# Layer 0's transfer queue reordered: third context and batch 1's queries and keys first, X and the loads for the layer's end later

## The chip, the cores and the metric

The kernel runs on one core of one Trainium2 chip. The metric is device time in microseconds (us) of one launch. The core has five instruction streams: PE (TensorE: matmuls; its weight loads are listed apart as PEld), DVE (VectorE), ACT (ScalarE), POOL (GpSimd) and SP (SyncE), which here issues all transfers. A transfer issued by SP is carried out by the core's 16 DMA engines; SP goes on at once, and whoever needs the data waits on a semaphore that the transfer raises when it has landed.

## The reference

Four layers of different kinds run one after the other on x (8 x 100 x 512), with one context ctx (8 x 361 x 512) for all. Only layer 0 is touched by this change. Cut to what matters:

```python
# layer 0: B = 8 batches, 32 query heads in 8 groups of 4, head size 16
q = x @ Wq + bq                       # (8, 100, 512)
k = ctx @ Wk + bk                     # (8, 361, 128)
v = ctx @ Wv + bv                     # (8, 361, 128)
scores = q . k / 4 + mask             # per batch and group: 4*100 query rows by 361 keys
attn = softmax(scores)
out = (attn . v) @ Wo + bo            # (8, 100, 512)
x = layernorm(out + x) * gamma + beta
# layers 1 to 3 (a recurrence, a cross attention, two cross attentions with an MLP) follow
```

## The kernel before, in words

`gqa_layer` is layer 0. Its attention is `grouped_attention`, the function that the change edits. It holds the projections' weights in SBUF, makes the queries of all eight batches at the start (`make_queries`, twelve units; high and low parts `qh` and `ql`, the low part kept in the memory of `outT`), and then runs over the batches b = 0 to 7.

A batch has 25 score tiles of 128 query rows (`TILES`), numbered n over all batches, i within one. Per tile PE makes the scores (L651 to L656), DVE adds the mask and takes the maximum (L550), ACT exponentiates (L474), PE transposes (L594), ACT or DVE copies the turned tile out of PSUM (L458, L298), and later PE multiplies with the values (L606, L613). Between the tiles of batch b, PE also makes the keys of batch b+1 (L575, at i = 1 to 4) and its values (L584, at i = 13 to 18), from `ctx`, which has two buffers: batch b's context is in `ctx[:, b % 2]`.

What orders the work around the change is SP's queue, written out by hand. SP executes its list in order, and where it says `wait_ge` everything behind waits too. Its helpers are:

- `load_context(b)` (L303) and `load_mask(b)` (L306): 724 KB and 722 KB from HBM.
- `store_queries(i)` (L357): writes the query parts of batch 0 (i = 0), batches 1 to 3 (i = 1) or 4 to 7 (i = 2) to HBM. `stack_queries(b)` (L312) reads six pieces of batch b's queries back into `qs`, stacked as the score matmul wants them.
- `stack_keys(b)` (L319, L324): waits for the keys of b (`k_done`), writes their two parts to HBM, **waits for these to land**, and reads six pieces back into `ks`.
- `store_output(b, quad)` (L332, L335): waits for `y_done`, writes half of the batch's output into `outT` and its row sums to HBM.
- `pack_sums(b)` (L340): waits until both halves have landed and reads the sums back as 128 x 25. DVE takes their reciprocal (`invert_sums`, L517), which stands in DVE's list between tiles i = 23 and 24 of batch b+1.
- `widen_inverse(b)` (L345, L351): waits for the reciprocals, writes them to HBM, waits for the landing, reads them back in eight broadcasts. POOL then scales the output rows (`scale_rows`, L422).

PE's first tile of a batch waits for that batch's `qs`, `ks`, and for `only_done`, two small products of POOL (L440).

Not part of the attention itself are `X` (the input rows, 1600 KB, needed for the residual sum after the attention) and `late`, four tiles for the layer's end:

```python
late = [(bias[:], a["L0_bo"]), (Wo[:], by_chunks(a["L0_Wo"])), (gamma[:], a["L0_gamma"]), (beta[:], a["L0_beta"])]
```

POOL adds the bias to `X` in eight pieces (L436), in its turn for b == 2, ahead of that batch's `only` products.

Of the kernel before, what the change touches and what calls it, by code (L numbers as in the profile page):

```python
# [12 lines left out]
B, L, C = 8, 100, 512  # L13
# [174 lines left out]
TILES = 1 + BLOCKS * KV0  # L188
# [6 lines left out]
def grouped_attention(nc, a, X, ident, columns, column, qh, ql, Wk, Wv, bv, heads_of, ctx, outT, late, last_out, queries, keys,  # L195
# [19 lines left out]
    with Scope(nc, "ga") as sc:  # L215
# [28 lines left out]
        query_out = [sc.sem(f"query_out{i}") for i in range(len(SPANS))]  # L244
# [56 lines left out]
        def _(sp):  # L301
            def load_context(b):
                sp.dma_start(ctx[:, b % 2], ctxT[b]).then_inc(ctx_in[b % 2], 16)  # L303

            def load_mask(b):
                sp.dma_start(maskb[:, b % 2], mask[b]).then_inc(mask_in[b % 2], 16)  # L306

            def stack_queries(b):
                for e in range(2):
                    for slot in range(SLOTS):  # L310
                        row = (e * SLOTS + slot) * D0
                        sp.dma_start(qs[row:row + D0, b % 2, :, e].bitcast(F32),  # L312
                                     queries[Q_PART[slot]].rearrange("(p e d) b n -> e d b p n", e=2, d=D0)[e, :, b]).then_inc(
                                         qs_in[b % 2], 16)

            def stack_keys(b):
                sp.wait_ge(k_done, b + 1)
                for part, k in enumerate((kh, kl)):
                    sp.dma_start(keys[b % 2, part], k[:, b % 2].bitcast(F32)).then_inc(keys_out[b % 2], 16)  # L319
                sp.wait_ge(keys_out[b % 2], 32 * (b // 2 + 1))  # L320
                for e in range(2):
                    for slot in range(SLOTS):
                        row = (e * SLOTS + slot) * D0
                        sp.dma_start(ks[row:row + D0, b % 2].bitcast(F32),  # L324
                                     keys[b % 2, K_PART[slot]].rearrange("(p e d) s -> e d p s", e=2, d=D0)[e]).then_inc(
                                         ks_in[b % 2], 16)

            def store_output(b, quad):
                sp.wait_ge(y_done, QUADS * b + quad + 1)
                for j in range(4):  # L330
                    row = (4 * quad + j) * D0
                    sp.dma_start(outT[row:row + D0, b].rearrange("d h l -> d (h l)"),  # L332
                                 y[32 * j:32 * j + D0, quad, :]).then_inc(y_out[quad], 16)
                if b + 1 < B:
                    sp.dma_start(row_sums[b, 4 * quad:4 * quad + 4, :], y[D0:P:32, quad, :]).then_inc(y_out[quad], 16)  # L335

            def pack_sums(b):
                for quad in range(QUADS):
                    sp.wait_ge(y_out[quad], 80 * (b + 1))
                sp.dma_start(packed[:, b % 2], row_sums[b].rearrange("g n -> (g n)").rearrange("(p k) -> p k", k=NS)).then_inc(  # L340
                    packed_in, 16)

            def widen_inverse(b):
                sp.wait_ge(inverse_done, b + 1)
                sp.dma_start(inverses[b].rearrange("g n -> (g n)").rearrange("(p k) -> p k", k=NS), inverse[:, b % 2]).then_inc(  # L345
                    inverse_out, 16)
                sp.wait_ge(inverse_out, 16 * (b + 1))
                if b >= 2:
                    sp.wait_ge(scaled, b - 1)
                for g in range(KV0):  # L350
                    sp.dma_start(wide[g * D0:(g + 1) * D0, b % 2], inverses[b, g:g + 1].broadcast_to([D0, HG * L])).then_inc(wide_in, 16)  # L351

            def store_queries(i):
                first, end = SPANS[i]
                sp.wait_ge(query_low, CC * (i + 1))
                for part, q in enumerate((qh, ql)):
                    sp.dma_start(queries[part, :, first:end, :], q[:, first:end].rearrange("p b c l -> p b (c l)").bitcast(F32)).then_inc(  # L357
                        query_out[i], 16)
# [17 lines left out]
            load_context(1)  # L376
            load_mask(1)
            store_queries(1)
            sp.dma_start(X, a["x"].rearrange("b l c -> l b c")).then_inc(X_in, 16)
            store_queries(2)  # L380
            for tile, source in late:
                sp.dma_start(tile, source).then_inc(late_in, 16)
            for i in (1, 2):
                sp.wait_ge(query_out[i], 32)
            sp.wait_ge(tails_kept, 4)
            for b in range(B):
                if b and b + 1 < B:
                    sp.wait_ge(masked_done, TILES * b)
                    load_mask(b + 1)
                if b + 1 < B:  # L390
                    if b:
                        sp.wait_ge(score_full, TILES * b)
                    stack_queries(b + 1)
                if b:
                    store_output(b - 1, 0)
                if b + 1 < B:
                    stack_keys(b + 1)
                if b:
                    store_output(b - 1, 1)
                    pack_sums(b - 1)  # L400
                if b + 2 < B:
                    sp.wait_ge(value_full, b + 2)
                    load_context(b + 2)
                if b:
                    widen_inverse(b - 1)
            store_output(B - 1, 0)
            store_output(B - 1, 1)
            sp.wait_ge(late_in, 16 * len(late))
# [1 line left out]
        @block.gpsimd  # L410
        def _(pool):
            nc.gpsimd.memset(qs[:].bitcast(F32), 0.0).then_inc(stack_clear, 1)

            def keep_tails(first, end, units):
                pool.wait_ge(query_low, units)
                for part, q in enumerate((qh, ql)):
                    nc.gpsimd.tensor_copy(tail[:, part, first:end], q[:, first:end, HG - 1, L - LEFT:L].bitcast(F32)).then_inc(tails_kept, 1)

            def scale_rows(b):
                rows = outT[:, b].rearrange("p h l -> p (h l)")  # L420
                pool.wait_ge(wide_in, 16 * KV0 * (b + 1))
                nc.gpsimd.tensor_tensor(rows, rows, wide[:, b % 2], ALU.mult).then_inc(scaled, 1)  # L422

            pool.wait_ge(heads_in, 16)
            for b in range(B):
                if b == 0:
                    keep_tails(0, 1, CC)
                    pool.wait_ge(tails_kept, 2)
                if b == 1:
                    keep_tails(1, B, len(UNITS))  # L430
                    pool.wait_ge(tails_kept, 4)
                if b == 2:
                    pool.wait_ge(X_in, 16)
                    pool.wait_ge(late_in, 16 * len(late))
                    for i in range(B):
                        nc.gpsimd.tensor_tensor(X[:, i, :], X[:, i, :], late[0][0], ALU.add).then_inc(biased, 1)  # L436
                if b >= 2:
                    pool.wait_ge(score_full, TILES * (b - 2) + 1)
                for part in range(2):
                    nc.gpsimd.tensor_tensor(only[:, b % 2, part],  # L440
                                            tail[:, part, b:b + 1, :].broadcast_to([P, KV0, LEFT]),
                                            heads_of[:].rearrange("p (g a) -> p g a", a=1).broadcast_to([P, KV0, LEFT]),
                                            ALU.mult).then_inc(only_done, 1)
                if b >= 2:
                    scale_rows(b - 2)
            scale_rows(B - 2)
# [1565 lines left out]
class Heads:  # L2012
# [51 lines left out]
    def load_context(self, sp, n):  # L2064
        if n >= 2:
            sp.wait_ge(self.y_full, CC * (n - 1))
        b, rows = n % B, STILES[2][1]
        sp.dma_start(self.x[:, n % 2, :, 0:2].bitcast(F32), self.ctx_parts[b, :, :, 0:2]).then_inc(self.x_in[n % 2], 16)
        sp.dma_start(self.x[0:rows, n % 2, :, 2].bitcast(F32), self.ctx_parts[b, 0:rows, :, 2]).then_inc(self.x_in[n % 2], 16)
# [1052 lines left out]
```

## Time and profile before

| | us |
|---|---|
| Time before, median of 3 runs | 2667.86 |
| lowest and highest of the 3 | 2667.09, 2668.03 |
| the profiled execution's own time | 2664.75 |
| its span, first to last instruction | 2663.0 |
| PE busy in the span | 2457.7 (92%) |
| DVE, ACT, POOL busy | 1385.2, 1151.1, 753.3 |

Layer 0's attention takes roughly the first 270 us of the span. All positions in time below are us from the start of the span. In a timeline a row gives the start, the duration, the engine (SPq is SP's queue of issued transfers, the duration then that of the issuing), the line in the kernel, what is written from what, and in brackets how long the engine was idle before and who ended that.

### The profile page before, as it was taken

What the parts mean: (1) busy time and instruction counts of PE and PEld (TensorE: products, weight loads), DVE (VectorE), ACT (ScalarE), POOL (GpSimd) and SP (SyncE); (2) the same over time, 40 slices, a digit from 0 to 9 for tenths busy, and PEclk for the clock granted to TensorE, in tenths of its full rate; (3) what the DMA queues carried; (4) which work ended last, traced back from release to release, by engine and by line L of the source; (5) the groups of instructions that cost most, each with busy time, mean ns of one, the idle gap of its engine ahead of it and who ended that gap; (6) DMA issues with size and microseconds to landing.
All of it is one profiled execution on the core that took longest, in us unless ns stands there. A gap on an engine that the chain in (4) does not pass through costs nothing. (4 is left out here: it accounts for less than half of the span.)

```text
span 2663.0 us, 37768 instructions
## 1 busy us (share of the span) xinstructions
PE 2457.7 (92%) x13976; PEld 2162.7 (81%) x13976; DVE 1385.2 (52%) x2360; ACT 1151.1 (43%) x2473; POOL 753.3 (28%) x386
## 2 busy tenths in 40 slices
PE   7998689989999689899899999979999999999698
PEld 5675434479896457799899999979998999999698
DVE  4666631278885633233366665633334556664632
ACT  3786212233333432223476666622246666664320
POOL 1100322252220450442143342406204243431300
PEclk9999879999998799899999999999999999999799
DMA  7552253589994157434876665625287566663300
GB/s 234 131 135 67 84 211 113 135 249 237 240 234 154 67 179 241 143 137 158 298 238 211 202 208 177 196 86 184 107 298 254 189 205 215 218 198 110 115 16 25
DMA packets 237306, 459.14 MB, mean 172 GB/s; under 512 B 90588, under 2 KB 133620, under 8 KB 236356
## 3 DMA queue, kind: packets, MB, share of 16 engines
q1 hardware_dynamic: 237124, 456.73, 55.2%
q8 instruction: 112, 1.84, 0.3%
q14 instruction: 70, 0.57, 0.1%
HBM read 345.46 MB, written 119.37 MB: 175 GB/s over the span
## 5 line engine op out<-in xcount | busy, mean ns | idle before, releaser
L2007 PE MATMUL att_ring<-ca_pp,att_arena 128*128 128x400 f32 (+1 forms) x2304 | 431.3, 345 | 11.3 <-issue 9.0
L2007 PEld LDWEIGHTS att_ring<-ca_pp,att_arena 128*128 128x128 f32 (+1 forms) x2304 | 417.6, 189 | 18.1 <-issue 17.9
L2077 POOL TENSOR_TENSOR att_arena<-att_arena 128x1448 fp32r<-128x1448 f32 x64 | 212.3, 3317 | 611.7 <-ACT att_arena L2084 611.7
L2007 PE MATMUL att_ring<-att_arena,qk_wh 128*128 128x362 f32 x1024 | 256.4, 332 | 0.0
L2693 DVE TENSOR_TENSOR ca_yl<-att_ring,att_arena 128x400 fp32r<-128x400 f32 x256 | 146.6, 573 | 189.0 <-ACT att_arena L2651 189.0
L2007 PE MATMUL att_ring<-att_arena,qk_wl 128*128 128x362 f32 x512 | 173.2, 338 | 18.5 <-POOL att_arena L2264 18.2
L2007 PEld LDWEIGHTS att_ring<-att_arena,qk_wh 128*128 128x128 f32 x1024 | 185.5, 192 | 0.0
L2651 ACT ACTIVATE att_arena<-att_ring 128x400 fp32r<-128x400 f32 x256 | 128.8, 503 | 84.2 <-PE att_ring L2007 84.1
L2090 ACT ACTIVATE att_kstage<-att_score,att_shift 100x362 f32<-100x362 f32 x256 | 143.7, 562 | 43.4 <-DVE att_shift L2103 43.4
L1075 ACT ACTIVATE rec_stage<-rec_fbank,rec_columns 128x361 f32<-128x361 f32 x128 | 72.1, 563 | 197.3 <-PE rec_fbank L2007 196.6
L2007 PE MATMUL att_score<-att_arena 128*100 128x362 f32 x768 | 144.4, 338 | 0.0
L550 DVE CUSTOM_DVE_ANT_0 ga_masked<-ga_score,ga_maskb 128x361 f32<-128x361 f32 x200 | 103.4, 530 | 62.3 <-PE ga_score L656 52.3
L2007 PE MATMUL att_ring<-att_arena,ca_woh 128*128 128x400 f32 x512 | 135.0, 345 | 0.0
L2095 ACT ACTIVATE att_kstage<-att_kstage,att_share 100x362 f32<-100x362 f32 x256 | 132.2, 606 | 5.2 <-DVE att_share L2108 5.2
L2645 ACT ACTIVATE ca_pp<-att_ring 128x400 fp32r<-128x400 f32 (+1 forms) x192 | 83.0, 511 | 108.3 <-PE att_ring L2745 103.3
L2394 DVE TENSOR_SCALAR att_kstage<-att_ring,att_columns 128x361 f32<-128x361 f32 x64 | 37.9, 592 | 173.9 <-PE att_ring L2007 173.9
L2007 PEld LDWEIGHTS att_score<-att_arena 128*100 128x100 f32 x768 | 124.6, 169 | 1.1
L474 ACT ACTIVATE ga_probs<-ga_masked,ga_top 128x361 f32<-128x361 f32 x200 | 116.3, 595 | 15.5 <-DVE ga_top L550 15.3
L1161 DVE TENSOR_TENSOR_SCAN rec_work<-rec_wb,rec_work 128x1600 f32<-128x1600 f32 x32 | 117.8, 3682 | 2.6 <-DMA rec_wb<-kept_decay 2.6
L2101 DVE TENSOR_REDUCE att_top<-att_score 100x1 f32<-100x362 f32 x256 | 117.5, 521 | 1.2 <-PE att_score L2007 1.2
L2323 ACT ACTIVATE att_kstage<-att_ring,att_columns 128x361 f32<-128x361 f32 x64 | 36.1, 563 | 185.6 <-PE att_ring L2007 185.6
L2007 PEld LDWEIGHTS att_ring<-att_arena,qk_wl 128*128 128x128 f32 x512 | 98.3, 192 | 22.0 <-issue 11.8
(408 smaller groups left out, 5880.1 us busy)
## 6 DMA issues: line engine op xcount, KB each, us to landing
att_arena<-ctx_parts SPq DMA_DIRECT2D x64, 1024.0 KB, 5.9
att_arena<-keys SPq DMA_DIRECT2D x64, 724.0 KB, 5.2
att_arena<-ctx_parts SPq DMA_DIRECT2D x64, 420.0 KB, 7.0
queries<-att_arena SPq DMA_DIRECT2D x64, 400.0 KB, 6.7
att_arena<-queries SPq DMA_DIRECT2D x64, 400.0 KB, 4.0
keys<-rec_stage SPq DMA_DIRECT2D x32, 724.0 KB, 4.2
keys<-att_kstage SPq DMA_DIRECT2D x32, 724.0 KB, 3.2
l_arena<-kept_value SPq DMA_DIRECT2D x176, 100.0 KB, 5.7
```

The costliest lines, as they stand in the source:

```text
L474: nc.scalar.activation(probs[:, n % RP, 0:S], masked[:, n % RM, :], ACT.Exp, bias=top[:, n % RM:n % RM + 1], scale=-1.0).then_inc(exp_done, 1)
L550: nc.vector.tensor_tensor_reduce(masked[:, n % RM, :], score[n % RS][:, 0:S], maskb[:, b % 2, lb, :], -1.0, 3.0e38, ALU.add, ALU.min, top[ ...
L1075: nc.scalar.activation(stage[:, step % 2, h, 0:S], fbank[u % RING_F][:, 0:S], ACT.Identity, bias=column[:, i, group * G3 + h, 1:2]).then_i ...
L1161: nc.vector.tensor_tensor_scan(work[m % RING_W][:], wb[:, b % 2].rearrange("p j n -> p (j n)"), work[m % RING_W][:], 0.0, ALU.mult, ALU.ad ...
L2007: issued = nc.tensor.matmul(out, x, y, start=(first and k == 0), stop=(last and k == count - 1))
L2077: self.nc.gpsimd.tensor_tensor(self.kl[:, n % 2].bitcast(F32R), self.kl[:, n % 2], self.kh[:, n % 2].bitcast(F32), ALU.subtract).then_inc( ...
L2090: self.nc.scalar.activation(self.probs[:, n % 2, h, :], self.score[h][0:L, 0:SP], ACT.Exp, bias=self.shift[:, n % 2, h:h + 1], scale=float ...
L2095: self.nc.scalar.activation(self.probs[:, n % 2, h, :], self.probs[:, n % 2, h, :], ACT.Copy, scale=self.share[:, n % 2, h:h + 1]).then_in ...
L2101: self.nc.vector.reduce_max(self.top[:, n % 2, h:h + 1], self.score[h][0:L, 0:SP], AX_X).then_inc(self.top_done, 1)
L2645: nc.scalar.activation(pp[0:rows, i, 0, :], bank_of("turn", n, i)[0:rows, 0:G3 * L], ACT.Copy).then_inc(turn_high, 1)
L2651: nc.scalar.activation(yh[:, c, :, n % BH, :], bank_of("y", n, c)[:, 0:G3 * L].rearrange("p (h l) -> p h l", l=L), ACT.Copy).then_inc(y_hi ...
L2693: nc.vector.tensor_tensor(yl[:, c, :, n % BH, :], bank_of("y", n, c)[:, 0:G3 * L].rearrange("p (h l) -> p h l", l=L), yh[:, c, :, n % BH, ...
```

## The change

The queue of SP in `grouped_attention` is reordered, and POOL's addition of the bias moves from its turn for b == 2 to that for b == 4. No transfer and no arithmetic is added or removed.

```diff
             store_queries(1)
-            sp.dma_start(X, a["x"].rearrange("b l c -> l b c")).then_inc(X_in, 16)
+            sp.wait_ge(value_full, 1)
+            load_context(2)
+            sp.wait_ge(query_out[1], 32)
+            stack_queries(1)
             store_queries(2)
-            for tile, source in late:
-                sp.dma_start(tile, source).then_inc(late_in, 16)
-            for i in (1, 2):
-                sp.wait_ge(query_out[i], 32)
+            stack_keys(1)
+            sp.wait_ge(query_out[2], 32)
             sp.wait_ge(tails_kept, 4)
-            for b in range(B):
-                if b and b + 1 < B:
+            for b in range(1, B):
+                if b + 1 < B:
                     sp.wait_ge(masked_done, TILES * b)
                     load_mask(b + 1)
-                if b + 1 < B:
-                    if b:
-                        sp.wait_ge(score_full, TILES * b)
+                    sp.wait_ge(score_full, TILES * b)
                     stack_queries(b + 1)
-                if b:
-                    store_output(b - 1, 0)
+                if b + 2 < B:
+                    sp.wait_ge(value_full, b + 1)
+                    load_context(b + 2)
+                store_output(b - 1, 0)
                 if b + 1 < B:
                     stack_keys(b + 1)
-                if b:
-                    store_output(b - 1, 1)
-                    pack_sums(b - 1)
-                if b + 2 < B:
-                    sp.wait_ge(value_full, b + 2)
-                    load_context(b + 2)
-                if b:
-                    widen_inverse(b - 1)
+                store_output(b - 1, 1)
+                pack_sums(b - 1)
+                widen_inverse(b - 1)
+                if b == 1:
+                    sp.dma_start(X, a["x"].rearrange("b l c -> l b c")).then_inc(X_in, 16)
+                if b == 2:
+                    for tile, source in late:
+                        sp.dma_start(tile, source).then_inc(late_in, 16)
@@ POOL
-                if b == 2:
+                if b == 4:
                     pool.wait_ge(X_in, 16)
                     pool.wait_ge(late_in, 16 * len(late))
```

On SP, from the end of the query stores of batches 1 to 3 up to the loads for batch 2, the list before reads as follows (the row numbers are left out here and below; x6 stands for six pieces).

```order
L379 DMA state_X<-in_x 100x8x512
L357 DMA l_queries<-l_qh 128x1600
L357 DMA l_queries<-l_outT 128x1600
L382 DMA l_bias<-in_L_bo 100x512
L382 DMA l_Wo<-in_L_Wo 128x4x512
L382 DMA l_gamma<-in_L_gamma 100x512
L382 DMA l_beta<-in_L_beta 100x512
L312 DMA ga_qs<-l_queries 16x4x400 x6
L319 DMA l_keys<-ga_kh 128x362
L319 DMA l_keys<-ga_kl 128x362
L324 DMA ga_ks<-l_keys 16x4x362 x6
L303 DMA l_ctx<-in_ctxT 128x1448
```

The changed kernel has this at the same place.

```order
L303 DMA l_ctx<-in_ctxT 128x1448
L312 DMA ga_qs<-l_queries 16x4x400 x6
L357 DMA l_queries<-l_qh 128x1600
L357 DMA l_queries<-l_outT 128x1600
L319 DMA l_keys<-ga_kh 128x362
L319 DMA l_keys<-ga_kl 128x362
L324 DMA ga_ks<-l_keys 16x4x362 x6
L306 DMA ga_maskb<-in_mask 128x1444
L312 DMA ga_qs<-l_queries 16x4x400 x6
L303 DMA l_ctx<-in_ctxT 128x1448
```

X and the four late loads are gone from here, context 2 stands first, and batch 1's queries now go ahead of the last query store.

Further on, SP's list of the changed kernel passes from its loop's turn for b = 1 to that for b = 2 like this; before, the rows L345, L351, L306 and L312 stood there without the X row, and context 4 (L303) stood further on, behind the next L340.

```order
L340 DMA ga_packed<-l_row_sums 128x25
L345 DMA l_inverses<-ga_inverse 128x25
L351 DMA ga_wide<-l_inverses 16x400 x8
L403 DMA state_X<-in_x 100x8x512
L306 DMA ga_maskb<-in_mask 128x1444
L312 DMA ga_qs<-l_queries 16x4x400 x6
L303 DMA l_ctx<-in_ctxT 128x1448
L332 DMA l_outT<-ga_y 16x400 x4
L335 DMA l_row_sums<-ga_y 4x400
L319 DMA l_keys<-ga_kh 128x362
L319 DMA l_keys<-ga_kl 128x362
L324 DMA ga_ks<-l_keys 16x4x362 x6
```

X now stands directly ahead of mask 3, the queries of batch 3, context 4 and the keys of batch 3; the four late loads stand in the same way ahead of mask 4 one turn later. The next context has moved from behind the packed sums to a place ahead of the outputs and keys, in every turn.

On POOL, the changed kernel's list has the bias addition (L437) here; before, it stood ahead of the third pair of `only` products, before any scaling.

```order
L441 TENSOR_TENSOR ga_only<-ga_tail,l_heads_of 128x128 x2
L423 TENSOR_TENSOR l_outT<-l_outT,ga_wide 128x400
L437 TENSOR_TENSOR state_X<-state_X,l_bias 100x512 x8
L441 TENSOR_TENSOR ga_only<-ga_tail,l_heads_of 128x128 x2
L423 TENSOR_TENSOR l_outT<-l_outT,ga_wide 128x400
```

It has moved behind the scaling of batch 1 and stands directly ahead of the `only` products of batch 4.

## Rows read from the trace of the kernel before

**Rows 1.** PE's timeline: first tiles of batches 0 to 3, batch 0's last.

```profile
63.29 0.49 PE L594 MATMUL ga_turn<-state_ident,ga_probs 128*128 128x128 f32 x3
71.06 0.64 PE L651 MATMUL ga_score<-ga_kh,ga_only 128*128 128x362 f32 x1 [7.28 <-issue]
...
98.37 0.41 PE L651 MATMUL ga_score<-ga_kh,ga_only 128*128 128x362 f32 x1
...
123.14 0.41 PE L651 MATMUL ga_score<-ga_kh,ga_only 128*128 128x362 f32 x1
```

**Rows 2.** SP's timeline, 32 to 72 us.

```profile
32.66 0.41 SPq L379 DMA_DIRECT2D state_X<-in_x  x1
42.75 0.33 SPq L357 DMA_DIRECT2D l_queries<-l_qh  x1
...
43.59 0.36 SPq L382 DMA_DIRECT2D l_bias<-in_L_bo  x1
...
45.54 2.55 SPq L382 DMA_DIRECT2D l_beta<-in_L_beta  x1
54.49 2.67 SPq L312 DMA_DIRECT2D ga_qs<-l_queries  x6
...
65.24 2.66 SPq L324 DMA_DIRECT2D ga_ks<-l_keys  x6
```

**Rows 3.** Windows: busy us of PE, PEld, DVE, ACT, POOL, then clock, DMA share, GB/s.

```profile
36.00:39.50 3.50, 3.50 (x12) 1.98 (x11) 0.73 (x2) 1.19 (x2) 0.00 (x0) 1.00 1.00 400
...
40.00:43.00 3.00, 1.60 (x6) 0.70 (x5) 0.67 (x2) 0.59 (x1) 0.21 (x1) 1.00 0.67 141
...
107.50:110.50 3.00, 3.00 (x47) 1.92 (x44) 1.55 (x5) 1.83 (x5) 0.00 (x0) 1.00 1.04 193
...
71.00:76.00 5.00, 4.94 (x38) 3.86 (x39) 1.08 (x4) 1.95 (x4) 2.50 (x4) 0.50 1.05 307
```

**Rows 4.** Transfers with KB and median us from issue to landing: the last query stores.

```profile
l_queries<-l_outT SPq DMA_DIRECT2D x1, 800.0 KB, 11.3
```

**Rows 5.** SP's timeline, 98 to 158 us: the turns for b = 2 and b = 3.

```profile
98.61 0.32 SPq L345 DMA_DIRECT2D l_inverses<-ga_inverse  x1
...
103.69 0.42 SPq L306 DMA_DIRECT2D ga_maskb<-in_mask  x1
...
114.49 2.66 SPq L324 DMA_DIRECT2D ga_ks<-l_keys  x6
...
122.08 0.34 SPq L340 DMA_DIRECT2D ga_packed<-l_row_sums  x1
122.46 0.43 SPq L303 DMA_DIRECT2D l_ctx<-in_ctxT  x1
124.02 0.32 SPq L345 DMA_DIRECT2D l_inverses<-ga_inverse  x1
...
130.42 0.42 SPq L306 DMA_DIRECT2D ga_maskb<-in_mask  x1
...
140.75 2.66 SPq L324 DMA_DIRECT2D ga_ks<-l_keys  x6
...
150.88 0.32 SPq L345 DMA_DIRECT2D l_inverses<-ga_inverse  x1
...
157.35 0.42 SPq L306 DMA_DIRECT2D ga_maskb<-in_mask  x1
```

**Rows 6.** DVE's timeline: batch 1's keys, and the end of batch 2.

```profile
48.67 0.59 DVE L493 SCALAR_TENSOR_TENSOR ga_kl<-ga_front,ga_bk,ga_kh 128x362 fp32r<-128x362 f32 x1 [0.75 <-ACT ga_kh L455]
...
123.68 0.31 DVE L517 RECIPROCAL ga_inverse<-ga_packed 128x25 f32<-128x25 f32 x1 [0.55 <-DMA ga_packed<-l_row_sums]
```

**Rows 7.** PE's timeline: the first key product in batch 3.

```profile
126.64 0.88 PE L575 MATMUL ga_front<-l_ctx,l_Wk 128*128 128x362 f32 x2 [1.42 <-DMA l_ctx<-in_ctxT]
```

**Rows 8.** POOL's timeline: the bias addition.

```profile
62.94 9.84 POOL L436 TENSOR_TENSOR state_X<-state_X,l_bias 100x512 f32<-100x512 f32 x8 [18.81 <-DMA l_beta<-in_L_beta]
```

**Rows 9.** Waits of all engines, 0 to 300 us: us in total, times, longest.

```profile
DVE ga_inverse L517 <- DMA ga_packed<-l_row_sums: 4.1, 5, 1.7
```

## Prediction

> **What bounds the kernel now.** I read PE's timeline first, since PE is the busiest engine, and looked for the places in layer 0's attention where it stands still. Batch 0's last rows end at 63.29 + 0.49 = 63.8, and batch 1's first tile starts at 71.06: a gap of 7.3 us [rows 1]. It is the largest hole in the attention. SP's timeline says what was late: the six reads that bring batch 1's keys were issued at 65.24, and the first tile came 5.8 us after that. They were late because batch 1's queries were issued only at 54.49, and those because SP stood behind the last query stores, which had been queued behind X: issued at 43.1, they landed 11.3 us later [rows 2, 4]. After the gap the granted clock was 0.50 from 71 to 76 us, the lower of its two levels, 1.2 GHz [rows 3]. So batch 1 lasted 98.37 - 71.06 = 27.3 us, and batch 2, at full clock, 123.14 - 98.37 = 24.8 [rows 1].
>
> The second reading matters more. From batch 2 on, who sets the pace? A turn of SP's loop took 130.42 - 103.69 = 26.7 and 157.35 - 130.42 = 26.9 us, while PE can do a batch in 24.8 [rows 1, 5]. In DVE's timeline the reciprocal of batch 1's sums waits for the packed sums (0.55 us), and in the list of waits this happens 5 times, 4.1 us together [rows 6, 9]. Everything that DVE has behind it, the masking of the next tiles first, waits too. That closes a ring: SP stores outputs and keys and packs the sums; DVE, held by them, makes the inverse; SP widens it and starts the next turn. SP's ring is the bound from batch 2 to 6, by about 2 us a batch. PE's wait of 1.42 us for context 4, issued at 122.46 right behind the packing, lies inside the same slack [rows 5, 7]: PE catches up until DVE holds it.
>
> So the sum must be made along this ring, and the marks are the issues of the inverse store: 98.61, 124.02, 150.88 [rows 5].
>
> **The change part by part.**
>
> *Batch 1's queries and keys first.* The DMA engines were full until 39.5 and fell to a share of 0.67 in 40 to 43, when X moved alone, so the query stores of batches 1 to 3 have landed at about 40 [rows 3]. SP then issues batch 1's queries (2.7 us, to about 43.3) and the last stores by 44.1. The keys are ready at 48.67 + 0.59 = 49.3 [rows 6]. Even if the last stores took the old 11.3 us, to 55.4, the key reads could go out at about 56 and batch 1 start 5.8 later, at 62, still before PE's 63.8. The gap goes whole, and with it the slow clock: 7.3 + 2.5 (27.3 - 24.8) = 9.8 us. The first inverse moves from 98.61 to 88.8. **Term a: -9.8.**
>
> *X behind the first widening.* SP's own issue costs 0.41 [rows 2]. What counts is what is queued behind it: mask 3, queries 3, context 4, two outputs, and then the key store, whose landing SP waits for. Before, that landing stood 114.49 - 103.69 = 10.8 after the mask's issue [rows 5]. How long X takes is not in one row. From below: 1.64 MB at the 400 GB/s of full engines is 4.1 us. From above: at the 141 GB/s that it had alone, 11.6 [rows 3]. The last query stores, 1.64 MB behind it, landed at 54.4; at 400 GB/s they take 4.1, so the engines that X kept longest were free by about 50, 9.5 to 10 us after X began at 40 [rows 3, 4]. I take 9.5. Then the chain behind X's issue: 1.6 for a small transfer's latency (packing issued 122.08, used at 123.68 [rows 5, 6]), 9.5 for X, mask 0.74 MB at 400 GB/s 1.85, queries 0.61 MB at 193 GB/s 3.2 [rows 3], context 1.85, outputs 0.4, keys 0.37 MB at 400 GB/s 0.9: 19.3 in place of 10.8. **Term b: +8.5** (3.1 to 10.6).
>
> A share of 0.67 with nothing else to move is 10.7 engines of 16: X seems to use only some of them, and whatever needs all 16 waits for these [rows 3]. The Trainium skill (DMA: Bandwidth & Descriptors, "Why a DMA increments its semaphore by 16 and not by 1") says why: the number of engines is the largest up to 16 that divides the slowest dimension, which for 100 rows is 10. By its 27 GiB/s per engine X would take an estimated 5.6 us, and the total below would be +2.3 instead of +6.2; the trace's 141 GB/s is half of that rate, and the measurement decides.
>
> *The late loads one turn later.* Four issues, 1.6 MB, in the same place. From below 4.2 us at 400 GB/s; from above, beta landed at 62.94 (POOL's start) when the stores before it had landed at 54.4: 8.5, with other traffic mixed in [rows 4, 8]. Three of the four have 100 rows like X, the largest (Wo) 128. I take 6. The chain is 1.6 + 6 + 1.85 + 3.2 + 1.85 + 0.4 + 0.9 = 15.8 in place of 140.75 - 130.42 = 10.3. **Term c: +5.5** (3.7 to 8.0).
>
> *The context ahead of outputs and keys, each turn.* Before, its issue (0.43) was hidden behind the packing's landing. Now 1.85 us of traffic stands ahead of the key store that SP waits for. Turns b = 2 and 3 have it in b and c; in b = 4 and 5 it costs between nothing (the key store is issued late enough) and 1.85. The chain without it comes to 8.0 against 10.3 measured, so it partly fits; I take 1.0 each. **Term d: +2.0** (0 to 3.7). PE's waits for context go, for which I credit nothing, since DVE is held by the sums right after.
>
> *Bias on POOL at batch 4.* Inverse 1 would be issued at 88.8 + 25.4 + 8.5 = 122.7, the first late load 6.4 later at 129.1, landed by 136.7. POOL's 9.84 us [rows 8] end at 146.5, with batch 4's `only` products right behind. Batch 4's key reads go out at 129.1 + 15.8 = 144.9 and serve it at 150.7. POOL is hidden by about 3 us. Cost nothing; without that cover each us late is a us.
>
> Sum: -9.8 + 8.5 + 5.5 + 2.0 = **+6.2 us**. Against the profiled execution's own 2664.75 that is 2671.0; this execution lies 3.1 under the median of its runs, 2667.86, so against that median I forecast **2674.1**. In words: the hole at batch 1 is filled, but X and the late loads cost the ring more than that later, where before they ran while PE stood still for the keys anyway or beside work with slack.
>
> **The rivals.**
>
> *All later loads are hidden, the gain stays.* If the engines take key stores past X, or if SP's waits have more slack than I see, b is 0.4 and c is 2.1 (the issues alone), d nothing: -7.3 us, 2660.6. For it: the DMA share over the attention is far from full, and X leaves a third of the engines idle. Against: SP's ring had no slack in five turns [rows 9]. It decides where the keys of batch 3 land within 11 us of mask 3's issue. 0.17.
>
> *X and late spread evenly over the engines.* The low ends: -9.8 + 3.1 + 3.7 + 0 = -3.0 us, 2664.9. 0.20. The page's count of 10 engines with its rate, worked out above, falls between this case and the forecast.
>
> *The high ends*, or POOL's bias late on top: -9.8 + 10.6 + 8.0 + 3.7 = +12.5 us, 2680.4. For it: X's own rate alone. 0.12.
>
> *The gap doesn't go*, because batch 1's key store is stuck behind the query stores until after 58: a is near nothing and the rest is paid, about +14. The margin of 2 us under the worst landing speaks against it. 0.04.
>
> *The forecast*, +2 to +10 us around +6.2: 0.47.
>
> **How the numbers follow.** About 0.2% (5.3 us) is what a measurement of this kernel can tell from no change. Of the forecast's 0.47, which straddles that bound, 0.33 lies above it and 0.14 within. With the high ends and the gap that stays, slower is 0.33 + 0.12 + 0.04 = 0.49. Faster is 0.16 of the hidden rival and 0.02 of the even spread: 0.18. The rest, 0.33, is within. Both signs being likely, the range reaches from just above the hidden rival to the high ends: 2661 to 2680; the forecast's own is 2670 to 2678.
>
> **What would show it.** Right: batch 1's first tile at about 63.8 with no clock below 1.00 after it; the first inverse store near 88.8; in the turn with X, some 19 us from X's issue to the key reads, PE idle for most of 9 us between batches 2 and 3 with a dip of the clock, which costs nothing since SP is later still; inverse 2 near 155, behind the old 150.88; DVE's wait for packed sums grown from 4.1 us to over 12; no PE wait for context from batch 3 on. Wrong: key reads in the turns of X and late no later than 11 us after the mask's issue (the gain then stays), or batch 7's first tile earlier than before. If batch 4 starts right after POOL's bias addition, POOL has taken the ring's place.

## The result, and the profile after

The changed kernel takes 2676.38 us (median of 6 runs, 2674.2 to 2686.24) against 2667.05 for the one before, measured beside it. The ratio is 1.0042, 95% interval 1.0029 to 1.0055: slower by 11 us, between 8 and 15. The forecast was 2674.1 us, range 2661 to 2680, with slower the likeliest at 0.49. The profiled executions are single ones: the one before lies 2.3 us below the median of its comparison runs, so differences of 2 to 5 us between the positions of two profiles are no more than these executions vary by.

The profiled execution has a span of 2673.4 us, 10.4 more than before, at the same work:

```profile
span 2673.4 us, 37768 instructions
PE 2461.5 (92%) x13976; PEld 2166.1 (81%) x13976; DVE 1381.0 (52%) x2360; ACT 1149.7 (43%) x2473; POOL 752.8 (28%) x386
```

PE's timeline, at the first tiles of batches 1, 3 and 4 (L652 is L651 of before, moved by a line), answers to [rows 1]:

```profile
64.27 0.41 PE L652 MATMUL ga_score<-ga_kh,ga_only 128*128 128x362 f32 x1
...
125.00 0.64 PE L652 MATMUL ga_score<-ga_kh,ga_only 128*128 128x362 f32 x1 [10.93 <-issue]
...
158.77 0.64 PE L652 MATMUL ga_score<-ga_kh,ga_only 128*128 128x362 f32 x1 [7.15 <-DMA ga_ks<-l_keys]
```

The 7.3 us gap at batch 1 is gone. In its place PE stands still for 10.9 us ahead of batch 3 and for 7.2 us ahead of batch 4, where it did not wait before. SP's timeline says why. The marks are the inverse stores (L345), one each turn, and answer to [rows 5]:

```profile
89.29 0.34 SPq L345 DMA_DIRECT2D l_inverses<-ga_inverse  x1
...
94.44 0.36 SPq L403 DMA_DIRECT2D state_X<-in_x  x1
...
103.83 0.53 SPq L319 DMA_DIRECT2D l_keys<-ga_kl  x1
119.14 2.66 SPq L324 DMA_DIRECT2D ga_ks<-l_keys  x6
...
128.13 0.34 SPq L345 DMA_DIRECT2D l_inverses<-ga_inverse  x1
...
133.19 0.36 SPq L406 DMA_DIRECT2D l_bias<-in_L_bo  x1
...
153.11 2.66 SPq L324 DMA_DIRECT2D ga_ks<-l_keys  x6
...
162.10 0.34 SPq L345 DMA_DIRECT2D l_inverses<-ga_inverse  x1
...
189.15 0.34 SPq L345 DMA_DIRECT2D l_inverses<-ga_inverse  x1
...
282.61 0.41 SPq L1581 DMA_DIRECT2D l_query_weight<-in_L_w_q  x1
```

The reader is to see the wait between the key store and the key reads: 119.14 - 104.36 = 14.8 us in X's turn, where it was 2.3 before. The first mark is 9.3 us earlier than the old 98.61. The second, old 124.02, is 4.1 later; the third, old 150.88, 11.2 later. From there the difference stays: the last row, SP's first load after the attention, stood at 270.93 before and is 11.7 later.

DVE's timeline and the list of waits show who passes this on to the tiles, and answer to [rows 6, 9]:

```profile
127.79 0.31 DVE L518 RECIPROCAL ga_inverse<-ga_packed 128x25 f32<-128x25 f32 x1 [13.97 <-DMA ga_packed<-l_row_sums]
```

```profile
DVE ga_inverse L518 <- DMA ga_packed<-l_row_sums: 33.1, 5, 14.0
```

DVE's wait for packed sums has grown from 4.1 to 33.1 us. Everything behind it in DVE's list, the masking of the next tiles, waits with it.

The windows show the DMA engines while X moves beside mask, queries and context, and then PE's idle stretch (columns as in [rows 3]):

```profile
97.00:101.00 4.00, 4.00 (x53) 2.21 (x53) 2.60 (x8) 2.84 (x8) 0.54 (x2) 1.00 0.98 226
101.00:105.00 4.00, 4.00 (x35) 3.97 (x35) 3.75 (x13) 3.98 (x10) 0.00 (x0) 1.00 1.06 134
114.00:123.00 9.00, 0.07 (x1) 0.00 (x0) 0.00 (x0) 0.95 (x3) 0.00 (x0) 0.74 0.52 137
123.00:129.00 6.00, 4.00 (x37) 3.42 (x37) 1.21 (x5) 0.47 (x1) 0.00 (x0) 0.53 0.21 31
```

With all engines busy they move 134 to 226 GB/s, not the 400 that full engines moved in [rows 3]. The clock falls to its lower level within PE's idle stretch and stays there until about 129 (0.53 from 123 to 129). PE has next to nothing to lose by it, as DVE is held until 127.8.

### The profile page after: what moved, and what is told of

Its sections match the earlier page's. It is cut to its first block and busy times, and to the rows that moved or that the text cites. A ratio compares the mean times of both kernels' runs of the same rounds, so it can differ in the third digit from the quotient of the medians.

```text
span 2673.4 us, 37768 instructions
## 1 busy us (share of the span) xinstructions
PE 2461.5 (92%) x13976; PEld 2166.1 (81%) x13976; DVE 1381.0 (52%) x2360; ACT 1149.7 (43%) x2473; POOL 752.8 (28%) x386
## 5 line engine op out<-in xcount | busy, mean ns | idle before, releaser
L2008 PEld LDWEIGHTS att_ring<-ca_pp,att_arena 128*128 128x128 f32 (+1 forms) x2304 | 415.8, 188 | 15.9 <-issue 15.8
L2008 PEld LDWEIGHTS att_ring<-att_arena,qk_wl 128*128 128x128 f32 x512 | 98.1, 192 | 21.8 <-issue 12.0
```

Of the source, the lines that this page charges most:

```text
L2008: issued = nc.tensor.matmul(out, x, y, start=(first and k == 0), stop=(last and k == count - 1))
```

## Experiments

In each, the marks are those above; the mark at the attention's end is SP's load of l_query_weight (before 270.93, changed 282.61). Ratios are to the kernel before, run beside each.

**1. The two late groups of loads taken out of the loop's middle.**

```diff
-                if b == 1:
+                if b == 6:
                     sp.dma_start(X, ...)
-                if b == 2:
                     for tile, source in late: ...
# POOL: the bias addition moves behind the loop, ahead of scale_rows(B - 2)
```

> The changed kernel with X and the late loads issued at the end of the turn b = 6, when no masks, queries or keys are to follow, and the bias added by POOL ahead of its last scaling; transfers unchanged, 100 rows each. Theory (terms b and c are all that the change costs): the first inverse store stays near 89.3 us, the following marks come every 25.5 to 27 us (114.7, 141, 168, 195, 221), PE doesn't stand still between batches 2 and 3, and the kernel is 5 to 8 us faster than the one before, 2659 to 2662 us; a few us may be given back because batch 6's outputs land behind X. Rival (filling the gap at batch 1 is worth nothing, since the ring runs at its own pace whatever stands ahead): 2667 or more.

Ratio 1.0002 (0.9992 to 1.0013), 2667.38 us. The marks:

```profile
88.56 0.34 SPq L345 DMA_DIRECT2D l_inverses<-ga_inverse  x1
...
116.14 0.34 SPq L345 DMA_DIRECT2D l_inverses<-ga_inverse  x1
...
143.05 0.34 SPq L345 DMA_DIRECT2D l_inverses<-ga_inverse  x1
...
225.85 0.34 SPq L345 DMA_DIRECT2D l_inverses<-ga_inverse  x1
...
233.34 3.97 SPq L405 DMA_DIRECT2D l_beta<-in_L_beta  x1
...
253.97 0.36 SPq L345 DMA_DIRECT2D l_inverses<-ga_inverse  x1
```

The turns b = 2 and 3 fall from 38.8 and 34.0 us to 27.6 and 26.9: the loads did cost the turns in which they stood. But no gain over the kernel before remains, which the theory had at 5 to 8 us; by its time alone this run lies where the rival had it (2667 or more). The marks say where the gain went: the first one keeps its 10 us, the last turn, where X and the late loads now stood ahead of batch 6's outputs, took 28.1 in place of 21.4, and the turns b = 2 to 6 sum to 137.3 us against 132.6 before. Of this last difference most can be the two executions: this one took 2669.14, 1.8 above its median, and the one before lies 2.3 below. Experiment 8 decides against the rival.

**2. X alone where the change puts it.** Only the late loads go to the end of b = 6; the bias addition moves behind POOL's loop as in experiment 1.

```diff
                 if b == 1:
                     sp.dma_start(X, ...)
-                if b == 2:
+                if b == 6:
                     for tile, source in late: ...
```

> The changed kernel with X where the change puts it, and only the late loads moved on to the end of the turn b = 6 (bias ahead of POOL's last scaling): term b without term c. Theory: the turn b = 2 still takes 38 to 39 us, the turn b = 3 falls from 34.0 to 27; 4 to 7 us faster than the changed kernel, 2669 to 2672 us. Rival (the ring's slack after X hides the late loads): no difference, 2675 or more.

Ratio 1.0011 (1.0001 to 1.0021), 2669.2 us. First marks 88.26, 126.10, 153.41:

```profile
126.10 0.34 SPq L345 DMA_DIRECT2D l_inverses<-ga_inverse  x1
...
153.41 0.34 SPq L345 DMA_DIRECT2D l_inverses<-ga_inverse  x1
```

The turn with X takes 37.8 us, 10.3 more than in the first experiment; the next one takes 27.3. Term b without c, as the theory had it.

**3. The late loads alone.** X is issued behind batch 1's key reads.

```diff
             stack_keys(1)
+            sp.dma_start(X, ...)
             sp.wait_ge(query_out[2], 32)
...
-                if b == 1:
-                    sp.dma_start(X, ...)
```

> The changed kernel with X issued right behind batch 1's key reads, and the late loads left at the end of the turn b = 2: term c without term b. Theory: the turn b = 2 falls from 38.8 us to 27 to 28, the turn b = 3 stays at 33 to 34; 8 to 12 us faster than the changed kernel, 2664 to 2668 us. Rival (X costs about as much wherever it stands): 2672 or more.

Ratio 1.0004 (0.9995 to 1.0013), 2666.51 us.

```profile
116.99 0.34 SPq L345 DMA_DIRECT2D l_inverses<-ga_inverse  x1
...
150.79 0.34 SPq L345 DMA_DIRECT2D l_inverses<-ga_inverse  x1
```

The first mark is at 89.34 (changed kernel: 89.29), so X behind the keys moves it by nothing; the turn b = 2 takes 27.6 us and the one with the late loads 33.8, some 6.5 more than the 27.3 of experiment 2. The two terms are separate and add up.

**4. Is it the ten engines?** X, bias, gamma and beta are loaded as 96 and 4 rows (X's part of the edit is shown).

```diff
-                    sp.dma_start(X, a["x"].rearrange("b l c -> l b c")).then_inc(X_in, 16)
+                    for r0, r1 in ((0, 96), (96, L)):
+                        sp.dma_start(X[r0:r1], a["x"].rearrange("b l c -> l b c")[r0:r1]).then_inc(X_in, 16)
```

> The changed kernel with X, bias, gamma and beta each loaded in two transfers, rows 0 to 95 and rows 96 to 99, in place of one of 100 rows; nothing else moves. Theory (the ring of SP, DVE and POOL sets the pace, and a 100-row transfer keeps 10 of 16 engines far longer than its bytes need): X's turn, from the first inverse store to the second, falls from 38.8 us to 29 to 31, the late loads' turn from 34.0 to 30 or 31, and the kernel comes out 10 to 13 us faster than the changed one, at 2664 to 2667 us. Rival (the bytes cost it, however they are spread): both turns stay within 2 us and the time is 2674 to 2677.

Ratio 1.0023 (1.0011 to 1.0034), 2670.9 us. X's turn fell from 38.8 to 36.0 us and the late one from 34.0 to 33.4, between the two expectations, nearer the rival; the time lies midway between them, and its interval overlaps that of the changed kernel. The windows while X moves beside the rest:

```profile
98.00:100.00 2.00, 2.00 (x19) 0.94 (x14) 1.13 (x5) 1.37 (x3) 0.00 (x0) 1.00 1.05 217
100.00:102.00 2.00, 2.00 (x37) 1.79 (x37) 1.33 (x5) 1.44 (x4) 0.00 (x0) 1.00 1.07 233
```

The engines are full here as they were in the changed kernel (there the other transfers filled those that X left free), and they move 217 to 233 GB/s. That is what the changed kernel moved in the same stretch (226 from 97 to 101), so the even spread shows no higher rate. By the marks, spreading the rows is worth up to some 3 us; that most of X's cost is its bytes, and those behind it, at the rate that the mixture reaches, is read from these windows and has no run of its own.

**5. X by itself.**

```diff
                     sp.dma_start(X, ...)
+                    sp.wait_ge(X_in, 16)
```

> The changed kernel with SP waiting for X to land before it goes on to mask 3, so that X moves alone: this measures X's own duration. Theory (X's 10 engines are slowed by what the other six move beside it; in the changed kernel X seems to have taken 14 us): alone it takes 10 to 12 us from issue to landing, and mask, queries, context and keys then take the 10 to 12 us they take in a turn without X, so the key reads go out at 116 to 119 and the time stays within 3 us of the changed kernel. Rival (X takes 14 us by itself): the key reads go out at 120 or later and the kernel is 2 to 4 us slower still.

Ratio 1.0036 (1.0022 to 1.0049), 2673.98 us.

```profile
93.17 0.36 SPq L403 DMA_DIRECT2D state_X<-in_x  x1
106.45 0.36 SPq L306 DMA_DIRECT2D ga_maskb<-in_mask  x1
...
119.44 2.66 SPq L324 DMA_DIRECT2D ga_ks<-l_keys  x6
```

```profile
98.00:100.00 2.00, 2.00 (x39) 1.26 (x32) 1.08 (x5) 1.26 (x3) 0.00 (x0) 1.00 0.67 167
100.00:102.00 2.00, 2.00 (x20) 1.98 (x18) 1.99 (x8) 1.97 (x5) 0.00 (x0) 1.00 0.65 166
...
104.00:106.00 2.00, 2.00 (x19) 1.99 (x18) 1.49 (x5) 2.00 (x5) 0.00 (x0) 1.00 0.13 34
```

Alone X takes 13.3 us from issue until SP goes on, more than the 10 to 12 expected. It moves at about two thirds of the engines and 165 GB/s until shortly after 104, about 10 us of transfer; the rest is the way in and out. The key reads went out 26.3 us after X's issue, against 24.7 with everything queued at once. So the overlap with mask, queries and context saves only 1.6 us between these two executions: what moves beside X gains almost nothing from the third of the engines that X leaves free. The key reads at 119.44 fell between theory (119 at the latest) and rival (120 or later); the time stayed that of the changed kernel, as the theory had it.

**6. The contexts back in their old place**, in the changed kernel.

```diff
-                if b + 2 < B:
-                    sp.wait_ge(value_full, b + 1)
-                    load_context(b + 2)
                 store_output(b - 1, 0)
...
                 pack_sums(b - 1)
+                if b + 2 < B:
+                    sp.wait_ge(value_full, b + 1)
+                    load_context(b + 2)
```

> The changed kernel with load_context(b + 2) put back behind pack_sums(b - 1). Theory (term d small, of either sign): the key store lands 0 to 1.9 us earlier in each of the turns b = 1 to 5, while the landing of the inverse store takes 2.8 us again in place of 1.45; net within 3 us of the changed kernel, 2673 to 2679. Rival (the context's place matters, PE's waits for it of 1.4 to 1.9 us come back and count): 2680 or more.

Ratio 1.0027 (1.0018 to 1.0036), 2672.41 us, a little under the range expected; the interval overlaps that of the changed kernel. X's turn falls to 35.7 us and the late one to 32.4; the attention's end is at 278.25, 4.4 earlier than in the changed kernel:

```profile
124.98 0.32 SPq L345 DMA_DIRECT2D l_inverses<-ga_inverse  x1
...
157.42 0.32 SPq L345 DMA_DIRECT2D l_inverses<-ga_inverse  x1
...
278.25 0.41 SPq L1581 DMA_DIRECT2D l_query_weight<-in_L_w_q  x1
```

**7. The contexts ahead, alone, in the kernel before** (from b = 1 on).

```diff
+                if b and b + 2 < B:
+                    sp.wait_ge(value_full, b + 1)
+                    load_context(b + 2)
                 if b:
                     store_output(b - 1, 0)
...
                     pack_sums(b - 1)
-                if b + 2 < B:
+                if b == 0:
                     sp.wait_ge(value_full, b + 2)
                     load_context(b + 2)
```

> The kernel before with one part of the change alone: contexts 3 to 7 loaded ahead of the outputs and keys in each turn. Theory (the key store that SP waits for lands behind the context; putting the context back gave 4.3 us of marks in the changed kernel): PE's waits for context (1.4 to 1.9 us each) vanish, and yet the turns b = 2 to 5 grow by 0.5 to 1.5 us each, 2 to 5 us in all: 2668 to 2671. Rival (PE's waits for context counted): the kernel gets 2 to 6 us faster.

Ratio 1.0006 (0.9996 to 1.0016), 2666.07 us: between 1 us faster and 4 us slower. The rival, 2 to 6 us faster, is out; that it costs something, the theory's 2 to 5, isn't shown. The profile's attention ends at 274.85, 3.9 later, but this execution took 2668.56, 2.5 above its median. PE's waits for context are gone from the list of waits and DVE's for the sums are up from 4.1 to 17.6 us:

```profile
DVE ga_inverse L520 <- DMA ga_packed<-l_row_sums: 17.6, 5, 6.5
```

This is the plainest sign of the ring. A wait of PE was removed, and nothing was gained, because DVE's wait took its place. The other profiles bear it out: with the contexts behind and no load in the loop's middle (experiments 8 to 11) DVE's wait is 3.0 to 7.2 us, with the contexts ahead and no such load (experiment 1) 24.8.

**8. A place where X is hidden.** X goes behind batch 1's key reads, the late loads to the end of b = 6, the bias behind POOL's loop, contexts 3 to 7 in their old place. The stretch from 59 to 64 us was free: batch 1's keys had landed and mask 2 was not yet wanted.

> Batch 1's queries and keys first as in the changed kernel, context 2 too, but X issued right behind batch 1's key reads (at about 56 us, when the DMA engines would be idle until 65), the late loads at the end of the turn b = 6, the bias ahead of POOL's last scaling, and contexts 3 to 7 in their old place. Theory: X is hidden in the idle stretch and in the slack of the turn b = 1, so the first inverse store stays within 2 us of 89.3 and the turns after it last what they did before (25.4, 26.9, 26.5, 27.6, 26.1); at the end the late loads delay the packing of batch 6 by up to 3 us. Sum -9.3 + 2 = -7: 2658 to 2661 us. Rival (the ring gives every gain back): 2665 or more.

Ratio 0.9971 (0.9959 to 0.9984), 2657.74 us: 7.7 us faster than the kernel before, by its interval 4 to 11. The rival of this experiment and that of experiment 1, a ring that gives every gain back (2665 or more), is out.

```profile
55.28 0.41 SPq L385 DMA_DIRECT2D state_X<-in_x  x1
64.15 0.36 SPq L306 DMA_DIRECT2D ga_maskb<-in_mask  x1
...
78.42 2.67 SPq L324 DMA_DIRECT2D ga_ks<-l_keys  x6
...
88.60 0.32 SPq L345 DMA_DIRECT2D l_inverses<-ga_inverse  x1
...
266.63 0.41 SPq L1579 DMA_DIRECT2D l_query_weight<-in_L_w_q  x1
```

The key reads of batch 2 are only 0.8 us later than in the changed kernel (77.59), and the first mark doesn't move: the turn b = 1 has slack, because the inverse stands at DVE's tile 23 and SP reaches it early. The late loads at b = 6 cost 0.3 us (last turn 21.8 against 21.4).

**9. All later loads in that place**, bias at batch 2.

> As the run before it, but the late loads too are issued behind batch 1's key reads, right after X, and the bias is added at batch 2 again. Theory: X and the late loads take 16 to 19 us from 57, until 73 to 76, so that mask 2, queries 2 and the key store of batch 2 stand behind them; the keys of batch 2 land at 80 to 84 in place of 77.6 and the first inverse store at 90 to 94; nothing stands in the way later. Sum -9.3 + 0.7 to 4.5: 2659 to 2664 us. Rival: the turn b = 1 has no slack, first inverse store at 98 or later, no gain.

Ratio 0.9992 (0.9981 to 1.0003), 2663.32 us. Batch 2's key reads go out at 84.78, the first mark is at 94.04, as expected at its upper end: that is more than the slack of the turn b = 1 holds. By the interval no gain over the kernel before is shown.

**10. The same with 96 and 4 rows.**

> As the run before it, with X, bias, gamma and beta in two transfers of 96 and 4 rows, which gave 3.4 us in the changed kernel. Theory: the loads end 3 to 5 us earlier, the first inverse store is at 89 to 91, and the kernel is 7 to 9 us faster than the one before, 2657 to 2660 us. Rival (the loads were hidden already): no difference to the run with whole transfers.

Ratio 0.999 (0.9978 to 1.0002), 2660.01 us; key reads at 82.78, first mark at 92.64, later than expected, and the gain of 7 to 9 us that was expected didn't come. The interval overlaps that of experiment 9, so a difference isn't shown.

**11. Experiment 8 with 96 and 4 rows.**

> The version with X behind batch 1's key reads and the late loads at the end of the turn b = 6 (contexts in their old place), with X, bias, gamma and beta in transfers of 96 and 4 rows. Theory (both are hidden there already): within 2 us of the version with whole transfers, 2656 to 2660 us. Rival (the 10 engines still hold something up): 3 us or more faster.

Ratio 0.9969 (0.9957 to 0.9981), 2657.23 us: the same as experiment 8 within the intervals. Where the loads are hidden, how they are spread doesn't matter.

## Why the prediction was right, and where its terms were off

The direction and the mechanism held: the gap went, X and the late loads cost the ring more than it had been worth, and DVE's wait for the sums passed the cost on. The sizes held less well. The outcome lies nearer the high ends (+12.5) than the forecast's centre (+6.2), and the stated range covered faster, equal and slower alike, so that it was met proves little. The signs that were named came out as follows: batch 1's first tile at 64.27 (named 63.8), the first mark at 89.29 (88.8), PE idle 10.9 us between batches 2 and 3 (most of 9), DVE's wait 33.1 us (over 12), no wait of PE for context; but 24.7 us from X's issue to the key reads (some 19), and the third mark at 162.10 (near 155).

*The gap (term a, -9.8).* It went whole, and the clock stayed at full level there. The first mark moved by -9.3; in this execution SP's list was some 0.7 us late from the start on. Right.

*X (term b, +8.5).* The turn b = 2 grew by 38.8 - 25.4 = 13.4 us, above even the upper bound of 10.6. Experiments 1 and 2 set X's own share at 10.3; in the changed kernel, against the 27.6 us of the turn in experiment 3, it is 11.2. The rest, 2.2, is the context ahead and what a turn varies by itself. The step that failed is the chain "9.5 for X, mask 1.85, queries 3.2, context 1.85": X's 9.5 was right for its transfer alone (about 10, experiment 5), but mask, context and keys were costed at 400 GB/s and the queries at 193, each a rate from a window without such company. In the profile after, the sixteen engines moved 134 GB/s in one stretch of this chain, at a full share; the chain took 24.7 us, where the sum had 19.3. Share of DMA time is not rate.

*The ten engines.* The row with a share of 0.67 was read as X on some of the engines, and the Trainium skill's count (DMA: Bandwidth & Descriptors, "Why a DMA increments its semaphore by 16 and not by 1") agrees with it; X alone showed the same share in experiment 5. That 96 and 4 rows run on all sixteen no window shows by itself, since other transfers fill the rest. X's turn gained only 2.8 us by it. The rate per engine of the Trainium skill's page, from which 5.6 us for X had been estimated, isn't reached by these rows of 2 KB: 167 GB/s on two thirds of sixteen engines is about 16 GB/s each.

*The late loads (term c, +5.5).* 34.0 - 26.9 = 7.1 with the context ahead, within the bounds; 5.6 in experiment 6 with the context behind (32.4 against 26.9), 6.5 in experiment 3. Right in mechanism, 1.6 us small. That the miss was no larger is partly luck: from the first late load to the key reads it took 153.11 - 133.19 = 19.9 us, 4.1 more than the 15.8 of the sum, while the rest of the turn was 2.5 us shorter than before, with no context queued behind the packed sums. The sum had not counted that.

*The context's place (term d, +2.0).* The turns b = 4 and 5 changed by +0.5 and +1.2, the turn b = 6 by -1.3; together 0.5. The turn b = 5 also had a granted clock of 0.94 on average, where it was 1.00 before, so its +1.2 need not be the context's alone. In the kernel before, the context's place alone is worth between 1 us faster and 4 us slower (experiment 7). In the changed kernel, putting the context back brought the attention's end 4.4 us forward (experiment 6), with times whose intervals overlap. So its size stays open; that no wait of PE would be credited was right.

*POOL.* It added the bias from 144.91 to 154.82, and batch 4 started at 158.77 on its keys: hidden by 3.2 us, as forecast. The cover held though beta landed 8 us later than the forecast had it, because the keys were late by as much.

```profile
144.91 9.91 POOL L437 TENSOR_TENSOR state_X<-state_X,l_bias 100x512 f32<-100x512 f32 x8 [9.27 <-DMA l_beta<-in_L_beta]
154.79 0.75 POOL L441 TENSOR_TENSOR ga_only<-ga_tail,l_heads_of 128x128 fp32r<-128x128 f32 x2
```

The sum of the marks is -9.3 + 13.4 + 7.1 + 0.5 = +11.7, the forecast's +6.2; the span grew by 10.4, so later layers gave 1.3 back, which wasn't looked into. The rivals of hidden loads and of an even spread fell: the keys of batch 3 came 24 us after mask 3's issue, not 11.

What stays open: experiments 1 and 8 don't keep the whole first gain in their marks. In experiment 8 the turns b = 2 to 6 sum to 137.9 us against 132.6 before, with nothing of the change left in them; in experiment 11 to 133.5. The ring isn't what lengthened them, since DVE's wait for the sums was 3.9 us in all. Part of it is the clock: in experiment 8 it fell to 0.50 from about 200 to 206 us, behind a wait of PE for context 7 of 2.55 us, and from 145 to 148, behind one of 2.16, and these two turns (b = 6 and b = 4) are 3.6 of the 5.4 us longer. The kernel before had the same wait, 2.52 us, and kept the clock at 1.00. This execution also took 2662.11 us, 4.4 above its median. One profile of each can't tell a rule from the way these turns vary from run to run.

## What to carry to other kernels

Find out first whether a wait of the busiest engine lies on a ring that some queue closes each turn; a wait inside such a ring's slack is worth nothing, and a transfer moved into the ring ahead of a round trip that SP waits for is paid in full, whatever it used to be hidden by. A bulk load belongs where the queue waits for nothing behind it: here that was a free stretch of 5 us some 40 us earlier, with slack in the turn behind it for the rest of X's 10 us, and the same load there cost nothing in place of 10 to 11 us. Cost what stands behind a transfer by the rate of the mixture, from a window where such transfers run together, not by each one's best.

## What was not expected of the hardware

A DMA share of 1.0 covered rates from 134 to 400 GB/s in this kernel. X of 100 rows in pieces of 2 KB moved at 165 GB/s alone, at two thirds of the engines; with the transfers behind it, full engines moved 226 GB/s with whole rows of 100 and 217 to 233 with 96 + 4 rows. Letting X finish before anything else was queued lost only 1.6 us against queueing all at once (experiment 5, one execution of each). Why the mixture is so slow was not found.
